# Six denominator products a quad for eight, with two pair sums merged by an accumulating DMA

## The chip, the cores and the metric

One core of a Trainium2 chip runs the kernel. The metric is the device time of one execution in microseconds; the profile comes from one profiled execution of the same program.

## The reference

For each of 8 batches, `x` and `ctx` are 512 rows by 1024 columns. The kernel computes a gated cross attention over the 1024 columns with 16 heads of 32 rows each, and then a gated product whose operands are rounded to an 8-bit float:

```
x = x + tanh(g_xattn) * attention(layernorm(x), ctx, mask)       # 16 heads, softmax over the 1024 source columns
x = x + tanh(g_ffn) * (fp8(layernorm(x) * scale) / scale) @ (fp8(W2 * scale1) / scale1)
```

Inside the attention, `q`, `k` and `v` are projections with bias, the scores are divided by the root of 32, masked, and put through a softmax. Its denominator is the sum of the exponentials over all 1024 source columns.

## The kernel before, in words

A first stage (to about 570 us) projects every batch's `q`, `k` and `v` and stores them in DRAM. The second stage walks through 32 quads, `n`: four heads (128 rows) of one batch. A quad is a period of 64 slots, `k`. All five engines have the same list of slots written out by hand, and each does in a slot what the program lists for it.

- In slot `k` TensorE (PE) multiplies one 128 x 512 tile of scores (`scores`, L863) and one tile of unshifted scores for the maxima of the quad after it (`scores_for_max`, L878). ScalarE (ACT) takes the exponential of the first (`exp`, L715), VectorE (DVE) the maximum of the second (`maximum`, L1143). A slot's head is `k % 4`, and four slots make one chunk of 128 source columns. Slots 0 to 31 serve the first half of the target columns (`th` = 0), 32 to 63 the second.
- After every fourth slot (`k % 4 == 3`) PE multiplies a chunk of exponentials with `v` (`times_v`, L893).
- GpSimd (POOL) adds the chunks pairwise: pair `r` is made of the exponentials of slots 8r to 8r+7, one 128 x 512 addition for each head (`add_pair`, L398). Its four additions need the exponentials of slots 8r+4 to 8r+7. They go to one of two buffers of `pair_sum`.
- PE sums a pair's rows into the denominator's bank with a product by ones (`denominators`, L904): 4 instructions in the code, 8 records in the trace, one after every eighth slot: pair `r` at slot 19 + 8r, so pair 0 at slot 19, pair 1 at slot 27, pair 7 at slot 75, which is slot 11 of the period after.
- At slots 23 and 55 PE turns the maxima's negated high and low parts (`turn_max`, L933), ACT copies them and SyncE's queue (SP) sends them into the score operand (`set_max`), which the scores of slots 32 and 64 need. At slots 31 and 47 PE does the fp8 product of two quads before (`ffn`, L940).
- The inverse denominators go through SP's queue: `move_den`, the reciprocal on DVE (L1168, L1171), `move_inv`, `spread_inv`. POOL multiplies with them (`weigh`, L407) and adds the residual (`add_residual`, L413) behind pair 3. POOL also has one power of a single column (L427) behind pair 4.

## Time and profile before

| | |
|---|---|
| Median of 3 runs | 2501.88 us (2497.44 to 2505.27) |
| The profiled execution's own time | 2498.55 us |
| Its span | 2496.9 us |
| PE busy | 2441.7 us, 98% of the span |
| DVE busy | 1960.7 us, 79% |
| POOL busy | 1643.2 us, 66% |
| ACT busy | 1387.1 us, 56% |
| Mean granted TensorE clock | 0.996 |

Busy time is the union of an engine's instructions; matmuls overlap in the records, so a single record (0.40 us) is longer than the distance between two (0.23 us). The distances between starts are what a reader should take as PE's pace. POOL's issue of a DMA would not be counted as busy.

### The profile page before, as it was taken

To read this page: it belongs to the slowest core of one execution; us is meant where nothing else is said; L and a number is where in the kernel's file an instruction comes from. 1 tells how busy PE (TensorE), PEld (TensorE's weight loads), DVE (VectorE), ACT (ScalarE), POOL (GpSimd) and SP (SyncE) were. 2 spreads that over 40 slices of the span, in tenths; PEclk is the share of its full clock that TensorE was granted. 3 is DMA by queue.
4 is the path that set the end of the run, shared out by engine and by line. 5 is a ranking of instruction groups with operands and counts; after the bars stand their busy time and mean duration, and the time that the engine had idled before them with its cause. 6 is when DMAs were issued, how large, how long until landed. Compare 5 with 4: busy or idle time off the path is not lost.

```text
span 2496.9 us, 40504 instructions
## 1 busy us (share of the span) xinstructions
PE 2441.7 (98%) x13116; PEld 1382.0 (55%) x13177; DVE 1960.7 (79%) x3259; ACT 1387.1 (56%) x2606; POOL 1643.2 (66%) x1259
## 2 busy tenths in 40 slices
PE   7999999999999999999999999999999999999997
PEld 5888888875444444444444444444444444444442
DVE  6677776687788888888888888888888888888885
ACT  3333333315666666666666666666666666666664
POOL 2443333426777777777777777777777777777775
PEclk9999999999999999999999999999999999999999
DMA  6766666664444444444444444444444444444411
GB/s 245 262 243 237 234 235 235 227 188 100 94 102 98 102 101 102 97 94 95 94 93 100 92 92 92 92 92 101 92 93 95 99 101 102 98 101 97 104 45 56
DMA packets 241807, 313.48 MB, mean 126 GB/s; under 512 B 75000, under 2 KB 142648, under 8 KB 241624
## 3 DMA queue, kind: packets, MB, share of 16 engines
q1 hardware_dynamic: 230776, 275.56, 44.0%
q10 hardware_dynamic: 10848, 35.66, 4.0%
q8 instruction: 93, 1.52, 0.3%
q14 instruction: 90, 0.74, 0.1%
HBM read 199.83 MB, written 101.38 MB: 121 GB/s over the span
## 4 chain that ended last, share of the span: by engine, by line
PE 94%; DVE 1%; DMA 1%; issue 1%; POOL 1%; ACT 1%; SPq 0%; POOLq 0%; ACTq 0%; DVEq 0%
PE bank L863 22%; PE bank L893 20%; PE bank L848 20%; PE bank L878 19%; PE bank L904 9%; PE bank L940 4%; PE bank L933 1%; POOL pair_sum L398 1%; DMA q_st<-qx_scr 0%; DMA w_nat<-in_L_xattn_Wk_dram 0%; DMA v_scr<-stage 0%; ACT probs L715 0%; DVE x_raw L1043 0%; PE bank L802 0%; PE bank L924 0%
## 5 line engine op out<-in xcount | busy, mean ns | idle before, releaser
L398 POOL TENSOR_TENSOR pair_sum<-probs 128x512 f32<-128x512 f32 x1020 | 1279.2, 1286 | 399.0 <-ACT probs L715 399.0
L1143 DVE TENSOR_REDUCE part_max<-bank 128x1 f32<-128x512 f32 x2048 | 1276.6, 682 | 242.7 <-PE bank L878 229.2
L715 ACT ACTIVATE probs<-bank 128x512 f32<-128x512 f32 x2048 | 1067.4, 604 | 601.7 <-PE bank L863 578.7
L863 PE MATMUL bank<-q_st,k_st 100*128 100x512 f32 x2048 | 866.3, 425 | 6.0 <-ACT probs L715 6.0
L878 PE MATMUL bank<-k_st,q_st 98*128 98x512 f32 x2048 | 817.4, 399 | 8.3 <-DVE part_max L1143 6.5
L863 PEld LDWEIGHTS bank<-q_st,k_st 100*128 100x128 f32 x2048 | 387.4, 190 | 410.3 <-issue 211.2
L893 PE MATMUL bank<-probs,v_t 128*32 128x512 f32 x4096 | 545.6, 605 | 0.0
L878 PEld LDWEIGHTS bank<-k_st,q_st 98*128 98x128 f32 x2048 | 388.7, 190 | 129.2 <-DVE part_max L1143 15.8
L389 POOL TENSOR_TENSOR stage_lo<-stage,stage_hi 128x512 fp32r<-128x512 f32 x128 | 186.6, 1483 | 137.7 <-ACT stage_hi L661 136.2
L904 PE MATMUL bank<-pair_sum,ones 128*32 128x512 f32 x2040 | 265.5, 592 | 0.0
L661 ACT ACTIVATE stage_hi<-stage 128x512 fp32r<-128x512 f32 x128 | 80.2, 633 | 205.1 <-DVE stage L1007 142.9
L377 POOL TENSOR_TENSOR rstd<-ve,neg_half 128x4 f32<-128x4 f32 x8 | 14.6, 1830 | 230.7 <-DVE ve L1038 230.7
L893 PEld LDWEIGHTS bank<-probs,v_t 128*32 128x32 f32 x4096 | 80.8, 108 | 146.6 <-issue 92.8
L904 PEld LDWEIGHTS bank<-pair_sum,ones 128*32 128x32 f32 x2040 | 66.4, 110 | 152.5 <-issue 151.0
L1195 DVE SCALAR_TENSOR_TENSOR res<-bank,g,res 128x512 f32<-128x512 f32 x64 | 47.9, 750 | 112.3 <-PE bank L940 108.6
L940 PE MATMUL bank<-w2q,y_t 128*128 128x512 bf16 x435 | 103.9, 379 | 10.1 <-issue 9.6
L696 ACT ACTIVATE stage<-stage,sm_now 128x512 f32<-128x512 f32 x64 | 44.6, 720 | 119.3 <-DVE stage L1003 119.2
L848 PE MATMUL bank<-w_hi_v,c_hi 128*128 128x512 f32 x256 | 101.3, 396 | 4.2 <-DVE w_lo_q L1056 4.2
L848 PE MATMUL bank<-c_hi,w_hi_k 128*128 128x512 f32 x256 | 100.0, 390 | 1.4 <-DVE w_lo_k L1056 1.4
L848 PE MATMUL bank<-w_hi_v,c_lo 128*128 128x512 f32 x256 | 101.2, 395 | 0.0
L848 PE MATMUL bank<-w_lo_v,c_hi 128*128 128x512 f32 x256 | 100.8, 394 | 0.0
L848 PE MATMUL bank<-x_hi,w_hi_q 128*128 128x512 f32 x256 | 99.9, 390 | 0.0
(112 smaller groups left out, 2007.3 us busy)
## 6 DMA issues: line engine op xcount, KB each, us to landing
k_st<-k_scr SPq DMA_DIRECT2D x96, 512.0 KB
q_st<-q_scr SPq DMA_DIRECT2D x192, 256.0 KB
c_raw<-in_ctx_dram ACTq DMA_DIRECT2D x32, 512.0 KB, 7.0
k_scr<-stage_hi SPq DMA_DIRECT2D x64, 256.0 KB, 2.5
k_scr<-stage_lo SPq DMA_DIRECT2D x64, 256.0 KB, 2.7
v_scr<-stage SPq DMA_DIRECT2D x64, 256.0 KB, 2.9
q_scr<-stage_hi SPq DMA_DIRECT2D x64, 256.0 KB, 2.4
q_scr<-stage_lo SPq DMA_DIRECT2D x64, 256.0 KB, 2.7
```

What stands on the lines that cost most here:

```text
L389: nc.gpsimd.tensor_tensor(stage_lo[:, e % STG], stage[:, g % STG], stage_hi[:, e % STG].bitcast(F32), ALU.subtract).then_inc(qk_lo, 1)
L398: nc.gpsimd.tensor_tensor(pair_sum[:, r % 2, h], probs[:, a, h], probs[:, a + 1, h], ALU.add).then_inc(pair_done, 1)
L661: nc.scalar.activation(stage_hi[:, e % STG], stage[:, g % STG], ACT.Copy).then_inc(qk_hi, 1)
L715: nc.scalar.activation(probs[:, c % PR, h, :], s_bank_of(n, k)[:, :], ACT.Exp).then_inc(exp_done, 1)
L848: last = nc.tensor.matmul(acc, a, m, start=(cb == 0 and n == 0), stop=(cb == CB - 1 and n == 2))
L863: nc.tensor.matmul(s_bank_of(n, k)[:, :], k_st[p][0:KS, h, j * P:(j + 1) * P], q_st[p][0:KS, th, h, :], start=True, stop=True).then_inc(sc ...
L878: nc.tensor.matmul(x_bank_of(n, "tile", k)[:, :], q_st[p][0:KX, th, h, tc * P:(tc + 1) * P], k_st[p][0:KX, h, sh * HALF:(sh + 1) * HALF], ...
L893: last = nc.tensor.matmul(o_bank[D * h:D * (h + 1), :], v_t[p][:, j, D * h:D * (h + 1)], probs[:, c % PR, h, :], start=(j == 0), stop=(j = ...
L904: last = nc.tensor.matmul(d_bank[D * h:D * (h + 1), :], ones[:, :], pair_sum[:, r % 2, h, :], start=(i == 0), stop=(i == 3))
L940: last = nc.tensor.matmul(x_bank_of(n, f"ffn{half}", k)[:, :], y8_t[:, kc, :], w2q[:, kc, half * HALF:(half + 1) * HALF], start=(kc == 0), ...
L1143: nc.vector.tensor_reduce(part_max[:, th, sh, at:at + 1], x_bank_of(n, "tile", k)[:, :], AX, ALU.max).then_inc(max_done, 2)
L1195: nc.vector.scalar_tensor_tensor(res[p][:, s], x_bank_of(n, f"ffn{half}", k)[:, :], g2[:, 0:1], res[p][:, s], ALU.mult, ALU.add).then_inc( ...
```

## The change

- Denominators: six products for each quad and not eight. POOL issues a DMA that adds the sum of pair 0 onto that of pair 1 (and pair 4 onto pair 5), 128 rows of 2048 floats, in SBUF (`merge`). There are four buffers of sums now; the two new ones are the first stage's `stage` and `stage_hi`. The order is pair 2 at slot 27, the merged pair 0+1 at slot 35, pair 3 at slot 43, pair 6 at slot 59, the merged pair 4+5 at slot 67 (3 of the next period), pair 7 at slot 75 (11).
- The maxima's split: DVE's three small operations become reductions, with a copy on ACT (`minus_high`) between them, spread over slots 19 to 22 (51 to 54); the sign moves to the identity.
- The inverse's mask goes to POOL (`mask_inverse`), its gate factor to ACT (`mask_gates`); the reciprocal moves from slots 23 and 55 to 19 and 51. In SP's queue `set_max` stands ahead of `move_inv`, and the loads of `q` are split by half.
- On POOL the weighing is done in halves, behind pair 2 and behind pair 3; the power stands inside pair 5. The fp8 products stand at slots 39 and 51, and DVE's last two rounding steps at 27.

The core of the diff:

```diff
+            sums = [pair_sum[:, 0], pair_sum[:, 1], stage[:, :, :], stage_hi[:, :, :].bitcast(F32)]
...
-            F_JOBS = {23: "max1", 31: "ffn0", 47: "ffn1", 55: "max0"}
+            F_JOBS = {23: "max1", 39: "ffn0", 51: "ffn1", 55: "max0"}
+            DEN_AT = {27: 0, 35: 1, 43: 2, 59: 3}
+            DEN_AFTER = {3: 4, 11: 5}
+            NG = 6
+            SUM_OF_GROUP = (2, 1, 3, 6, 5, 7)
+            GROUP_OF_SUM = {1: 1, 2: 0, 3: 2, 5: 4, 6: 3, 7: 5}
+            MERGED = (0, 4)
...
-            FFN_AT = (31, 47)
+            FFN_AT = (39, 51)
...
+                    def wait_sum_free(n, r):
+
+                        m, was = (n, r - 4) if r >= 4 else (n - 1, r + 4)
+                        if m < 0:
+                            return
+                        if was in MERGED:
+                            pool.wait_ge(merged[was // 4], 16 * (m + 1))
+                        else:
+                            pool.wait_ge(den_done, NG * m + GROUP_OF_SUM[was] + 1)
...
                     def add_pair(n, r):
                         a = 2 * r % PR
-                        if counted(SJ * n + r - 1):
-                            pool.wait_ge(den_done, SJ * n + r - 1)
+                        wait_sum_free(n, r)
                         for h in range(QH):
+                            if (r, h) == (5, 1) and n > 0:
+                                invert_std_2(n - 1)
                             pool.wait_ge(exp_done, NSLOT * n + 2 * QH * r + QH + h + 1)
-                            nc.gpsimd.tensor_tensor(pair_sum[:, r % 2, h], probs[:, a, h], probs[:, a + 1, h],
+                            nc.gpsimd.tensor_tensor(sums[r % 4][:, h], probs[:, a, h], probs[:, a + 1, h],
                                                     ALU.add).then_inc(pair_done, 1)
...
+                    def merge(n, th):
+
+                        pool.wait_ge(pair_done, QH * (SJ * n + 4 * th + 2))
+                        pool.dma_start(sums[1], sums[0], accum_op=ALU.add).then_inc(merged[th], 16)
...
                     def period(n, p):
                         for r in range(SJ):
+                            if n == 0 and r == 0:
+                                wait_stage_free()
                             if real(n) and (n, r) != (LAST, SJ - 1):
                                 add_pair(n, r)
+                            if real(n) and r % 4 == 1:
+                                merge(n, r // 4)
+                            if r == 2 and ordinary(n - 1):
+                                mask_inverse(n - 1, 1)
+                                weigh(n - 1, 0)
+                            if r == 6 and real(n):
+                                mask_inverse(n, 0)
                             if r == 3 and ordinary(n - 1):
-                                weigh(n - 1)
+                                weigh(n - 1, 1)
                                 add_residual(n - 1, 1 - p)
...
-                    def denominators(m, r):
-                        th, i = r // 4, r % 4
+                    def denominators(m, g):
+                        th, i = g // 3, g % 3
+                        r = SUM_OF_GROUP[g]
                         if i == 0:
                             if counted(2 * m + th):
                                 pe.wait_ge(den_copied, 2 * m + th)
-                        pe.wait_ge(pair_done, QH * SJ * m + QH * (r + 1))
+                        if i == 1:
+                            pe.wait_ge(merged[th], 16 * (m + 1))
+                        else:
+                            pe.wait_ge(pair_done, QH * SJ * m + QH * (r + 1))
```

PE's program around slots 19 to 27, of before: the products with `v` after slot 23, the turn of the maxima, then the products with `v` after slot 27 and the denominator's. The slots' own tiles (L863, L878) are left out.

```order
L893 MATMUL bank3<-probs,v_t1 32x512 [waits exp_done]
L893 MATMUL bank3<-probs,v_t1 32x512 x3
L933 MATMUL bank6<-ident_r,neg_max 128x128 [waits max_done,negmax_done]
...
L893 MATMUL bank3<-probs,v_t1 32x512 [waits exp_done]
L893 MATMUL bank3<-probs,v_t1 32x512 x3
L904 MATMUL bank4<-pair_sum,ones 32x512 [waits pair_done]
L904 MATMUL bank4<-pair_sum,ones 32x512 x3
```

The same place of the change, from the products after slot 23 to the denominator's product at slot 27 and the one at slot 35.

```order
L989 MATMUL bank3<-probs,v_t0 32x512 [waits exp_done]
L989 MATMUL bank3<-probs,v_t0 32x512 x3
L1033 MATMUL bank6<-neg_ident,max_hl 128x128 [waits max_done,max_split]
...
L989 MATMUL bank3<-probs,v_t0 32x512 [waits exp_done]
L989 MATMUL bank3<-probs,v_t0 32x512 x3
L1004 MATMUL bank4<-stage,ones 32x512 [waits pair_done,den_copied]
L1004 MATMUL bank4<-stage,ones 32x512 x3
...
L1004 MATMUL bank4<-pair_sum,ones 32x512 [waits merged0]
L1004 MATMUL bank4<-pair_sum,ones 32x512 x3
```

At slot 27 stood the product of pair 1; now pair 2 (in `stage`) stands there, the first of its half. No product stands at slot 19 any more, and the one at slot 35 waits for the merging DMA.

POOL's program of before, from pair 2 of a period to pair 4:

```order
L398 TENSOR_TENSOR pair_sum<-probs 128x512 [waits exp_done,den_done]
L398 TENSOR_TENSOR pair_sum<-probs 128x512 [waits exp_done] x3
L398 TENSOR_TENSOR pair_sum<-probs 128x512 [waits exp_done,den_done]
L398 TENSOR_TENSOR pair_sum<-probs 128x512 [waits exp_done] x3
L407 TENSOR_TENSOR y<-o_raw,inv_b 128x1024 [waits inv_spread,o_copied]
L413 TENSOR_TENSOR res<-res,y 128x1024 [waits res_loaded0,norm_done]
L398 TENSOR_TENSOR pair_sum<-probs 128x512 [waits exp_done,den_done]
L398 TENSOR_TENSOR pair_sum<-probs 128x512 [waits exp_done] x3
L427 TENSOR_TENSOR rs<-ve,neg_half 128x1 [waits norm_done]
```

POOL's program of the change, from the end of pair 1 to the residual behind pair 3:

```order
L441 TENSOR_TENSOR pair_sum<-probs 128x512 [waits exp_done] x3
L447 DMA pair_sum<-pair_sum 128x2048 [waits pair_done]
L441 TENSOR_TENSOR stage<-probs 128x512 [waits exp_done,den_done]
L441 TENSOR_TENSOR stage<-probs 128x512 [waits exp_done] x3
L425 TENSOR_TENSOR inv_c<-inv_c,gtm_c 128x16 [waits gates_masked,inv_done]
L462 TENSOR_TENSOR y<-o_raw,inv_b 128x512 [waits inv_spread0,o_copied]
L441 TENSOR_TENSOR stage_hi<-probs 128x512 [waits exp_done,den_done]
L441 TENSOR_TENSOR stage_hi<-probs 128x512 [waits exp_done] x3
L462 TENSOR_TENSOR y<-o_raw,inv_b 128x512 [waits inv_spread1,o_copied]
L469 TENSOR_TENSOR res<-res,y 128x1024 [waits res_loaded0,norm_done,half_weighed]
```

The merging DMA is issued between pair 1 and pair 2, and the mask and the first half of the weighing come between pair 2 and pair 3.

## Rows read from the trace of the kernel before

**Rows 1.** Windows, steady stage: busy us by engine, clock, DMA share, GB/s

```profile
1000.00:1500.00 500.00, 496.56 (x2813) 245.38 (x2829) 408.84 (x717) 310.85 (x609) 381.62 (x294) 1.00 0.43 94
```

**Rows 2.** Waits of PE, whole span: total us, times, longest

```profile
PE bank L878 <- DVE part_max L1143: 6.5, 3, 5.0
```

**Rows 3.** The page's groups: busy, mean ns, idle before and its releaser

```profile
L398 POOL TENSOR_TENSOR pair_sum<-probs 128x512 f32<-128x512 f32 x1020 | 1279.2, 1286 | 399.0 <-ACT probs L715 399.0
L1143 DVE TENSOR_REDUCE part_max<-bank 128x1 f32<-128x512 f32 x2048 | 1276.6, 682 | 242.7 <-PE bank L878 229.2
L904 PE MATMUL bank<-pair_sum,ones 128*32 128x512 f32 x2040 | 265.5, 592 | 0.0
```

**Rows 4.** Timeline from slot 20 of one period: start, us, engine, line

```profile
1536.62 0.50 PE L863 MATMUL bank<-q_st,k_st 100*128 100x512 f32 x1
1537.24 2.06 ACT L715 ACTIVATE probs<-bank 128x512 f32<-128x512 f32 x4 [1.87 <-PE bank L863]
...
1537.98 5.02 POOL L398 TENSOR_TENSOR pair_sum<-probs 128x512 f32<-128x512 f32 x4 [1.98 <-ACT probs L715]
...
1539.68 0.33 PE L933 MATMUL bank<-ident_r,neg_max 128*128 128x128 f32 x1
...
1541.86 1.06 PE L893 MATMUL bank<-probs,v_t 128*32 128x512 f32 x8
...
1542.74 1.04 PE L904 MATMUL bank<-pair_sum,ones 128*32 128x512 f32 x8
1543.71 0.51 PE L863 MATMUL bank<-q_st,k_st 100*128 100x512 f32 x1
...
1547.01 1.67 PE L940 MATMUL bank<-w2q,y_t 128*128 128x512 bf16 x7 [0.16 <-issue]
```

**Rows 5.** Timeline, slots 60 to 64 (no denominator between) and slot 12

```profile
1515.66 0.50 PE L863 MATMUL bank<-q_st,k_st 100*128 100x512 f32 x1
...
1517.73 1.07 PE L893 MATMUL bank<-probs,v_t 128*32 128x512 f32 x8
1518.72 0.50 PE L863 MATMUL bank<-q_st,k_st 100*128 100x512 f32 x1
...
1529.63 0.50 PE L863 MATMUL bank<-q_st,k_st 100*128 100x512 f32 x1
...
1530.99 5.01 POOL L398 TENSOR_TENSOR pair_sum<-probs 128x512 f32<-128x512 f32 x4 [1.96 <-ACT probs L715]
```

**Rows 6.** Timeline, last period: POOL's additions, a waiting weight load, DVE

```profile
2440.36 4.97 POOL L398 TENSOR_TENSOR pair_sum<-probs 128x512 f32<-128x512 f32 x4 [1.38 <-ACT probs L715]
...
2445.49 0.13 PEld L904 LDWEIGHTS bank<-pair_sum,ones 128*32 128x32 f32 x4 [0.30 <-POOL pair_sum L398]
...
2463.16 7.41 POOL L398 TENSOR_TENSOR pair_sum<-probs 128x512 f32<-128x512 f32 x4 [2.64 <-ACT probs L715]
```

**Rows 7.** DMA issues: count, KB each, median us from issue to landing

```profile
v_t<-v_scr SPq DMA_DIRECT2D x32, 512.0 KB, 4.1
...
w_nat<-in_L_xattn_Wk_dram SPq DMA_DIRECT2D x1, 1024.0 KB, 10.3
```

**Rows 8.** Windows of 2 us inside the burst of loads

```profile
1524.00:1526.00 2.00, 2.00 (x13) 0.75 (x12) 1.97 (x4) 1.33 (x3) 1.99 (x2) 1.00 1.05 222
1526.00:1528.00 2.00, 2.00 (x12) 1.30 (x15) 1.45 (x3) 1.67 (x4) 2.00 (x3) 1.00 1.03 141
```

**Rows 9.** SP's own rows in that period: issue time of each DMA

```profile
1517.60 1.30 SPq L498 DMA_DIRECT2D k_st<-k_scr  x3
...
1531.36 0.56 SPq L518 DMA_DIRECT2D den_c<-den  x1
```

**Rows 10.** POOL's power of four columns, and DVE's small operation late once

```profile
L377 POOL TENSOR_TENSOR rstd<-ve,neg_half 128x4 f32<-128x4 f32 x8 | 14.6, 1830 | 230.7 <-DVE ve L1038 230.7
...
2431.71 0.57 DVE L1152 TENSOR_TENSOR row_max<-part_max 128x16 f32<-128x16 f32 x1
...
2432.32 0.17 DVE L1157 TENSOR_SCALAR neg_max<-row_max 128x16 fp32r<-128x16 f32 x1
```

More of the change, by code:

```diff
@@ L176, in flamingo_gated_layer @@
         init_done = sem("init_done")
-        stacked = [sem(f"stacked{i}") for i in range(TH)]
+        k_stacked = sem("k_stacked")
+        q_stacked = [sem(f"q_stacked{i}") for i in range(TH)]
         v_loaded = [sem(f"v_loaded{i}") for i in range(2)]
@@ L187, in flamingo_gated_layer @@
         pair_done = sem("pair_done")
+        merged = [sem(f"merged{i}") for i in range(TH)]
         pv_done = sem("pv_done")
@@ L193, in flamingo_gated_layer @@
         inv_done = sem("inv_done")
+        gates_masked = sem("gates_masked")
         inv_moved = sem("inv_moved")
-        inv_spread = sem("inv_spread")
+        inv_spread = [sem(f"inv_spread{i}") for i in range(TH)]
         tm_loaded = sem("tm_loaded")
         res_loaded = [sem(f"res_loaded{i}") for i in range(2)]
+        half_weighed = sem("half_weighed")
         norm_done = sem("norm_done")
@@ L588, in period @@
                             load_v(n + 1, 1 - p)
+                        if real(n) and real(n + 2):
+                            stack_q(n + 2, 0, p)
                         if real(n):
@@ L727, in copy_den, with minus_high @@
                         nc.scalar.activation(den[:, :], d_bank[:, :], ACT.Copy).then_inc(den_copied, 1)
+                    def minus_high(m, th):
+                        act.wait_ge(max_split, 4 * (2 * m + th) + 2)
+                        nc.scalar.activation(row_max[:, :, 1], max_hl[:, 0:QH * TC].bitcast(F32), ACT.Copy,
+                                             scale=-1.0).then_inc(max_split, 1)
                     def copy_max(n, m, th, k):
@@ L756, in normalize, with mask_gates @@
                                              scale=rss[:, 0:1]).then_inc(norm_done, 1)
+                    def mask_gates(m):
+                        act.wait_ge(tm_loaded, 16 * TH * (m + 1))
+                        if m == 0:
+                            act.wait_ge(chain_done, 1)
+                        if counted(4 * m):
+                            act.wait_ge(inv_done, 4 * m)
+                        nc.scalar.activation(gtm_c[:, :, :], tm_c[:, :, :], ACT.Copy, scale=g1[:, 0:1]).then_inc(gates_masked, 1)
                     def period(n, p):
@@ L761, in period @@
                                 exp(n, k)
+                            if k == 46 and real(n):
+                                mask_gates(n)
                             if k == 3 and ordinary(n - 1):
@@ L765, in period @@
                                 copy_den(n - 1, 1)
+                            if k == 20 and real(n):
+                                minus_high(n, 1)
+                            if k == 52 and real(n + 1):
+                                minus_high(n + 1, 0)
                             if k == 23 and real(n):
@@ L785, in _ @@
                     act.wait_ge(ident_done, 2)
-                    nc.scalar.activation(ident_r[:, :], ident_f[:, :], ACT.Copy).then_inc(ident_copied, 1)
+                    nc.scalar.activation(neg_ident[:, :], ident_f[:, :], ACT.Copy, scale=-1.0).then_inc(ident_copied, 1)
                     split_ctx(0)
```

196 lines of the change are left out of this document (112 added, 84 removed).

## The prediction

> **What bounds the kernel now.** I read the windows of the steady stage first: of 500 us PE is busy in 496.6, at a granted clock of 1.00 (its upper level, 2.4 GHz), DVE in 409, POOL in 382, ACT in 311 [rows 1]. The waits say the same from the other side: in the whole span PE waited 6.5 us for DVE's maxima, its longest wait for another engine's tiles [rows 2]. So in 32 periods PE sets the time: what leaves PE's list leaves the time, and what makes PE wait is added. POOL and DVE have room on average, but both run close to PE: POOL's groups wait 399 us in all for exponentials [rows 3], about 12 us a period, so a wait of PE for POOL would be decided by single slots.
>
> **What is removed.** One denominator product. From the products with `v` at slot 27 to the next slot's tile it is 1541.86 to 1543.71, 1.85 us, with a denominator between [rows 4], and 1517.73 to 1518.72, 0.99 us, without [rows 5]. So one costs PE 0.86 us. The page counts 2040 records, 255 products of 8 [rows 3]; two leave each of 32 quads, 64 in all: 64 x 0.86 = **-55.0 us**. The other products, the tiles and the fp8 products only change places.
>
> **The wait at slots 27 and 59.** The first product of each half is now that of pair 2 (pair 6). Its four additions follow the exponentials of slots 20 to 23, and it stands at slot 27. Before, pair 1 stood there, finished at 1530.99 + 5.01 = 1536.00 [rows 5], 6.7 us before PE came. In the row POOL starts pair 2 at 1537.98, 1.36 us behind slot 20's tile at 1536.62, and needs 5.02: it ends at 1543.00. PE came to the product at 1542.74 [rows 4]. Between slot 20 and slot 27 the change leaves PE's list as it was (4 + 4 slots, one turn), so PE comes as early as before, and must wait. From POOL's end to the weight load that waits there is the row of the last period: 2440.36 + 4.97 = 2445.33, load at 2445.49, 0.16 us [rows 6]; a load takes about 0.1. So the product starts at 1543.00 + 0.16 + 0.1 = 1543.26 for 1542.74, 0.5 us late. Slots 52 to 59 are the same list, so the same wait. It comes about 62 times (the last quad has no tiles beside it): 62 x 0.5 = **+31 us**. The bounds of this wait: 0.26 (POOL's end alone) gives +16, and 0.8, if the new reductions of the maxima or ACT's new copy hold the chain up a little, gives +50. DVE's last reduction of the split comes behind slot 22 for the turn after slot 23; if that is late by 0.1 or 0.2 us it is inside this wait, not beside it.
>
> **The issue of the merging DMA on POOL.** No DMA is issued from POOL before, so its price D is unknown. Behind pair 1 it delays pair 2. From slot 12 to slot 20 PE takes 1536.62 - 1529.63 = 6.99 us [rows 4, 5], less the 0.86 of slot 19's product: 6.13. POOL's four additions take 5.01 [rows 5], so 1.1 us are free and only D - 1.1 is added at slot 27. Below stands SP's issue, 1.30 us for three, 0.43 each [rows 9]; above, POOL's own slowest small operation, 1.83 us [rows 10]. I take 1.3, since software on POOL is nearer to the second, which adds 0.2 us in 31 periods: **+6 us**; the ends are 0 and 31 x 0.7 = +22. Behind pair 5 the fp8 product at slot 51 (at least 1.6 us [rows 4]) makes room for D and for the power, so nothing is added there. The Trainium skill (DMA: Bandwidth & Descriptors, Specifications) gives about 1 us to the first byte of a DMA issued from GpSimd; D by that would be under 1.1 and this term zero.
>
> **The merging DMA itself.** It starts when pair 1 is done, 1.36 + 5.01 = 6.4 us behind slot 12's tile. Slot 35's product comes at 6.13 + 6.12 + 0.5 + 0.98 + 6.0 = 19.7, so it may take 13.3 us with its issue. For pair 4+5: the additions and the power end 7.0 us behind slot 44, slot 67's product comes at 6.12 + 1.6 + 6.12 + 0.5 + 0.98 + 6.0 = 21.3: 14.3 us. It moves 1.05 MB and reads two such tiles. Rows for its price: 512 KB in 4.1 us, so 1 MB in 8; 1 MB among other loads in 10.3 [rows 7]; 2.1 MB read at the burst's 222 GB/s, 9.4 [rows 8]. The burst of the next quad's loads (issued from 1517.60 on, behind slot 63 [rows 9]) is 3.2 MB, 15 us at 222 GB/s and 23 at 141 [rows 8]; half of `q` is loaded later now, which leaves 2.4 MB, 11 to 17 us, over when pair 1 is done at slot 20, 18 us on. I take 10 to 11 us and **0 us**. The bounds: 8, and 3.15 MB (two reads, one write) at the burst's slow 141 GB/s, 22 us, which would cost (8.7 + 7.7) x 31 = +508. If cover is gone, each microsecond over both limits costs 62 us.
>
> **The rest, all at nothing.** DVE has 0.58 us free in four slots without a denominator (3.06 us from 1515.66 to 1518.72 [rows 5], less four maxima of 0.62 each), and its larger steps now stand at slots that keep a product (3, 11, 27, 43, 59) or an fp8 product. The reciprocal at slot 19 waits for `den_c`, issued at 1531.36, slot 13 to 14 [rows 9]; the loads ahead of it in the queue are now a quarter less, so it lands before slot 19. If not, DVE's maxima stop, and PE three tiles later. ACT has 1.0 us free in such a group (four exponentials in 2.06 [rows 4]) and gets one small copy at slots 20, 46 and 52. `set_max` now leaves earlier in SP's queue. POOL gets two masks and two halves for one weighing; after pair 2 they end before slot 28's exponential by my count, after pair 3 the residual makes pair 4 about 2 us late, and pair 5 catches up. The last period has no maxima, so PE is not full there and POOL's line decides: two issues, and the merged pair 4+5 which PE wants some 6 us after its issue and gets after 10. Part of that is covered by DVE's own backlog; I take **+4 us**, bounds 0 and 10.
>
> **Sum** against the profiled execution's own 2498.55 us: -55 + 31 + 6 + 0 + 4 = -14, so 2484.5. The median of the runs lies 3.3 us above that execution, so on its scale **2488 us**, a ratio of 0.994. What a measurement of this kernel can tell from no change is about 0.3%, 7.5 us.
>
> **The rivals.** *The merging DMA is too slow* (the other side). Place: slots 35 and 67. It decides from the point where both latenesses together eat 14/31 = 0.45 us a period, a duration of about 13.7 to 14 us; at 15 it is (1.7 + 0.7) x 31 = +74, 2562 us. For it: two reads, an arithmetic step nowhere seen in this trace. Against it: 1 MB in 8 to 10.3 [rows 7], and DMA engines busy 0.43 of the time on average [rows 1].
>
> *The issue is long*, D of 2.2 us or more, by its own work or by a lock. POOL's additions show that it can be held up: four took 7.41 us in the last period for 5 elsewhere [rows 6], while DVE worked on pairs of SBUF inputs, and DVE's 16-column operation took 0.57 us once, its neighbour 0.17 [rows 10]. At D = 2.2 the term is 31 x 1.1 = +34 for +6: 2516 us, slower. Against it: at slots 20 and 52 DVE has only maxima from PSUM and small reductions in its list. The Trainium skill (SBUF — State Buffer, Who interferes with whom) says that descriptors of a DMA issued from GpSimd starve while DVE runs in a two-port mode, and that reductions never contend on trn2; by that rule this case does not come up at these two slots.
>
> *No wait at slots 27 and 59*, because POOL's recorded ends, which the page calls rough, are late and its signal comes earlier, or a short D and the last period cost nothing: -55 + 0 to 15, 2450 to 2462 us. For it: that note. Against it: a waiting load of the last period came 0.16 us behind POOL's recorded end, not before it [rows 6].
>
> *It does nothing*: DVE or POOL takes over as the bound and fills the 1.7 us a period. For it: DVE 82% and POOL 76% busy [rows 1], of a shorter period 84% and 80% with the issues. Against it: both still wait. Time 2495 to 2505.
>
> **How the numbers follow.** My forecast, waits of half a microsecond twice a period and a hidden transfer: 0.52, its own range 2468 to 2508 (0.42 of it faster by over 0.3%, 0.08 within, 0.02 slower). No wait: 0.16, faster. Slow transfer: 0.13, slower. Long issue: 0.11, of which 0.02 within and 0.09 slower. Nothing: 0.08, of which 0.04 within, 0.02 either side. Faster 0.60, same 0.14, slower 0.26. The low end takes in most of the case without a wait, 2454; the high end the long issue and the mild part of a slow transfer, 2525.
>
> **What would show it.** Denominator records 1528 for 2040; PE's distance from `v`'s products to the next tile 0.99 us at slots 19 and 51. A wait of PE's weight load for POOL's additions of about 0.4 to 0.5 us, 62 times, and none for the merging DMA outside the last period. POOL's idle time ahead of pair 2 near zero. A period of about 58.9 us for 59.4 (16 x 3.06 + 8 x 0.86 + 2 x 1.6, and two turns of some 0.2). I am wrong if PE's waits name the DMA, if POOL starts pair 2 more than 0.3 us behind slot 20's exponential, or if PE waits for DVE at slots 20 to 24.

## The result and the profile after

The change makes the kernel slower: 2543.81 us median (2535.99 to 2553.53, 4 runs) for 2500.11 us (2497.44 to 2505.27, 4 runs) on the same chip, a ratio of 1.0174 with an interval of [1.0129, 1.0219]. The profiled execution took 2553.53 us, the longest of its four, with a span of 2551.7 us and a mean granted clock of 0.980. It lies 10 us above the median, so sums below are made against its own span.

First the windows of the steady stage, in the columns of [rows 1]: the first line answers to its line there, the others are three stretches of 3 us.

```profile
1000.00:1500.00 500.00, 485.08 (x2635) 238.92 (x2651) 396.86 (x690) 310.46 (x622) 389.32 (x328) 0.98 0.64 130
1326.00:1329.00 3.00, 3.00 (x8) 1.93 (x6) 1.39 (x4) 2.09 (x5) 1.92 (x2) 0.50 1.08 233
1329.00:1332.00 3.00, 3.00 (x12) 1.05 (x12) 1.28 (x3) 0.67 (x2) 3.00 (x3) 0.50 0.56 115
1332.00:1335.00 3.00, 3.00 (x20) 1.70 (x22) 2.40 (x5) 2.17 (x4) 0.23 (x2) 0.89 0.07 11
```

PE is no longer full: 485 us busy of 500, and even DVE has less to do in 500 us than before, so the whole line moves more slowly. The clock column reads 0.98. In the second and third line it is 0.50, the lower of its two levels (1.2 GHz for 2.4), although PE is busy in all 3 us. DMA went from 94 to 130 GB/s.

Lines picked from the waits over the whole span (us in total, times, longest) say for what PE, DVE, POOL and SyncE's queue wait:

```profile
DVE inv_c L1270 <- DMA den_c<-den: 41.2, 22, 4.3
PE bank L974 <- DMA k_st<-kx_scr: 21.0, 15, 1.9
PE bank L974 <- DVE part_max L1242: 20.0, 16, 4.8
POOL pair_sum L441 <- DMA q_scr<-stage_lo: 19.0, 1, 19.0
POOL pair_sum L447 <- POOL pair_sum L441: 18.8, 63, 0.3
PE bank L957 <- ACT probs L786: 17.4, 11, 14.1
PE bank L1004 <- POOL stage L441: 10.2, 19, 3.6
SPq L597 <- DMA inv_scr<-inv_c: 115.4, 63, 3.2
```

No wait of PE for the merging DMA is in the list. What PE waits for is the loads of `k` for the maxima's scores (L974), 15 times, and DVE's maxima, 16 times; DVE in turn waits 22 times at its reciprocal (L1270) for `den_c`. Before, PE waited for the maxima 3 times and 6.5 us [rows 2], and its list had no wait for `k_st`. The last line is of SyncE's queue, where the same wait of the inverse's spread was much shorter before:

```profile
SPq L528 <- DMA inv_scr<-inv_c: 22.5, 62, 1.7
```

The merging DMA, from the page (its issues, KB each, median us from issue to landing) and from its own line's view:

```profile
pair_sum<-pair_sum POOLq DMA_DIRECT2D x64, 1024.0 KB, 7.4
L447 POOL DMA_DIRECT2D pair_sum<-pair_sum x64: 867/884/1057, 603.1 to 2506.6; - x64
DMA to landing us min/median/max: 6.9/7.4/10.2
```

It holds POOL for 0.88 us, after a wait of 0.30 us for the pair before it, and lands after 7.4 us.

**Where the time went.** The turn of the maxima (L1033, L933 before) stands twice a period, behind slots 23 and 55, so the distances between its 64 starts are a ruler for the second stage. Read from those starts, with the stage cut at the third turn and at the last but one (60 halves between them), in us:

| kernel | start to third turn | 60 halves | rest | span |
|---|---|---|---|---|
| before | 617.4 | 1790.5 | 89.1 | 2496.9 |
| after | 633.5 | 1819.7 | 98.5 | 2551.7 |

So 16 us are lost ahead of the third turn, 29 in the steady stage and 9 at the end. Within the steady stage halves are of two kinds. Where nothing is late they take 27.58 us (slot 55 to 23) and 31.1 us (23 to 55), a period of 58.7 us for 59.7 by the same ruler: shorter, as forecast. The others are longer by up to 5 us. One of these is the half from the turn at 1298.88; the view of windows for it and for the half after it:

```profile
1298.88:1331.05 32.17, 30.10 (x157) 14.42 (x153) 24.40 (x41) 18.33 (x36) 23.32 (x21) 0.92 0.81 166
1331.05:1362.46 31.41, 31.09 (x172) 15.75 (x170) 23.75 (x44) 19.90 (x40) 24.23 (x21) 0.97 0.38 80
```

It takes 32.17 us where an undisturbed one takes 27.58, 4.6 us more, with 2.1 us of idle PE; the next one still has a clock of 0.97. Its chain of waits, in order of time (start, us, what):

```profile
1302.13 0.19 POOL inv_c L425
...
1302.34 3.25 DMA inv_scr<-inv_c
...
1305.61 0.56 SPq L597
...
1306.27 0.42 SPq L560
...
1307.68 16.45 DMA k_st<-kx_scr
...
1324.17 0.49 PE bank L974
```

and what POOL, PE and DVE show there on the timeline:

```profile
1323.92 0.88 POOL L447 DMA_DIRECT2D pair_sum<-pair_sum  x1 [0.30 <-POOL pair_sum L441]
1324.17 0.49 PE L974 MATMUL bank<-k_st,q_st 98*128 98x512 f32 x1 [1.93 <-DMA k_st<-kx_scr]
...
1326.01 0.63 PE L974 MATMUL bank<-k_st,q_st 98*128 98x512 f32 x1
...
1327.61 0.25 DVE L1270 RECIPROCAL inv_c<-den_c 128x16 f32<-128x16 f32 x1 [1.81 <-DMA den_c<-den]
```

POOL's mask of the inverse (L425) stands behind pair 6. SyncE's queue waits for it, sends the inverse to DRAM (3.25 us for 8 KB, where the same transfer took 1.4 us in the median before), then issues the spread (L597), and only behind that the loads of the next quad's `k` and `q` (L560): 7.4 us behind the turn. In the halves without loss it is 6.3 us, before it was 6.0. These loads land 1.9 us after PE wants them. Then PE runs at half clock, its matmul records 0.63 us for 0.40, to 1332: six microseconds at 0.50 are 3 us lost, more than the wait that went before. In 11 of the 30 periods the distance to the turn is 7.2 us or more (up to 7.7), and PE waits for `k_st` in each of them; in four others, issued at 6.3 to 6.9 us, it waits 0.6 to 1.2 us.

What made the chain late can be read from SyncE's rows. The kernel before, behind its turn at 1271.89:

```profile
1272.77 0.33 SPq L522 DMA_DIRECT2D inv_scr<-inv_c  x1
...
1274.19 0.54 SPq L528 DMA_DIRECT2D inv_b<-inv_scr  x1
1277.87 1.30 SPq L498 DMA_DIRECT2D k_st<-k_scr  x3
```

The change, behind its turn at 1298.88, has the maxima's transfer first:

```profile
1299.54 0.69 SPq L616 DMA_DIRECT2D q_st<-max_rows  x1
```

The inverse left 0.9 us behind the turn before and leaves 3.5 us behind it now (1302.34). The spread stood ahead of the loads in the kernel before too, with 3 us to spare. SyncE's queue waits for POOL's mask 56 times (115.7 us), so it is the mask's place behind pair 6, much more than the place of `set_max`, that made the inverse late; the second kernel below tells the two apart.

The clock did not fall behind every such wait. In after and in the second, fourth and ninth kernels below, all eight single waits of PE of 1.9 us or more in the 60 halves were followed by 3 to 10 us at 0.50; of those from 1.4 to 1.9 us some were and some were not (1.64 us at 1866.88 was, 1.76 us at 1746.60 was not).

### The profile page after: what moved, and what is told of

The parts are those of the page before. It is cut to its first block, busy times and chain, and to the rows that moved or that the text cites. A ratio compares the mean times of both kernels' runs of the same rounds, so it can differ in the third digit from the quotient of the medians.

```text
span 2551.7 us, 39827 instructions
## 1 busy us (share of the span) xinstructions
PE 2436.1 (95%) x12604; PEld 1374.4 (54%) x12665; DVE 1937.0 (76%) x3196; ACT 1406.7 (55%) x2702; POOL 1718.8 (67%) x1417
## 4 chain that ended last, share of the span: by engine, by line
PE 74%; DMA 9%; POOL 9%; issue 4%; DVE 2%; ACT 2%; SPq 1%; ACTq 0%; POOLq 0%; DVEq 0%
PE bank L942 20%; PE bank L957 16%; PE bank L989 14%; PE bank L974 13%; PE bank L1004 6%; POOL stage L441 6%; DMA den_c<-den 5%; PE bank L1040 4%; POOL pair_sum L441 3%; DMA k_st<-kx_scr 3%; ACT probs L786 1%; DMA q_scr<-stage_lo 1%; DMA inv_scr<-inv_c 0%; DVE part_max L1242 0%; DMA w_nat<-in_L_xattn_Wk_dram 0%
## 5 line engine op out<-in xcount | busy, mean ns | idle before, releaser
L786 ACT ACTIVATE probs<-bank 128x512 f32<-128x512 f32 x2048 | 1081.2, 603 | 634.7 <-PE bank L957 605.9
L957 PE MATMUL bank<-q_st,k_st 100*128 100x512 f32 x2048 | 876.9, 430 | 17.6 <-ACT probs L786 17.4
L974 PE MATMUL bank<-k_st,q_st 98*128 98x512 f32 x2048 | 829.0, 405 | 41.4 <-DMA k_st<-kx_scr 21.0
L441 POOL TENSOR_TENSOR pair_sum<-probs 128x512 f32<-128x512 f32 x512 | 642.2, 1283 | 184.9 <-ACT probs L786 165.8
L957 PEld LDWEIGHTS bank<-q_st,k_st 100*128 100x128 f32 x2048 | 392.9, 192 | 428.7 <-issue 226.8
L989 PE MATMUL bank<-probs,v_t 128*32 128x512 f32 x4096 | 554.9, 614 | 0.0
L974 PEld LDWEIGHTS bank<-k_st,q_st 98*128 98x128 f32 x2048 | 393.4, 192 | 172.6 <-DVE part_max L1242 44.0
L441 POOL TENSOR_TENSOR stage_hi<-probs 128x512 f32<-128x512 f32 x252 | 316.3, 1288 | 78.6 <-ACT probs L786 78.6
L441 POOL TENSOR_TENSOR stage<-probs 128x512 f32<-128x512 f32 x256 | 324.2, 1313 | 57.1 <-ACT probs L786 57.0
L390 POOL TENSOR_TENSOR rstd<-ve,neg_half 128x4 f32<-128x4 f32 x8 | 14.7, 1831 | 233.1 <-DVE ve L1137 233.1
L462 POOL TENSOR_TENSOR y<-o_raw,inv_b 128x512 f32<-128x512 f32 x62 | 80.0, 1291 | 79.7 <-DVE y L101 71.0
L1293 DVE SCALAR_TENSOR_TENSOR res<-bank,g,res 128x512 f32<-128x512 f32 x64 | 47.9, 750 | 103.4 <-PE bank L1040 98.2
```

The source lines that it names most:

```text
L441: nc.gpsimd.tensor_tensor(sums[r % 4][:, h], probs[:, a, h], probs[:, a + 1, h], ALU.add).then_inc(pair_done, 1)
L462: nc.gpsimd.tensor_tensor(y[:, th * HALF:(th + 1) * HALF], o_raw[:, th], inv_b[:, th], ALU.mult).then_inc(done, 1)
L786: nc.scalar.activation(probs[:, c % PR, h, :], s_bank_of(n, k)[:, :], ACT.Exp).then_inc(exp_done, 1)
L957: nc.tensor.matmul(s_bank_of(n, k)[:, :], k_st[p][0:KS, h, j * P:(j + 1) * P], q_st[p][0:KS, th, h, :], start=True, stop=True).then_inc(sc ...
L974: nc.tensor.matmul(x_bank_of(n, "tile", k)[:, :], q_st[p][0:KX, th, h, tc * P:(tc + 1) * P], k_st[p][0:KX, h, sh * HALF:(sh + 1) * HALF], ...
L989: last = nc.tensor.matmul(o_bank[D * h:D * (h + 1), :], v_t[p][:, j, D * h:D * (h + 1)], probs[:, c % PR, h, :], start=(j == 0), stop=(j = ...
```

## The experiments

Every kernel is compared with before on its own chip. The table holds all of them, each profiled execution cut as above; the rows are explained below.

| kernel | median us | ratio to before | to third turn | 60 halves | rest |
|---|---|---|---|---|---|
| after | 2543.8 | 1.0174 [1.0129, 1.0219] | 633.5 | 1819.7 | 98.5 |
| buffer wait later (e1) | 2539.0 | 1.0158 [1.0141, 1.0175] | 630.6 | 1802.4 | 98.1 |
| mask earlier (e2) | 2516.1 | 1.0060 [1.0043, 1.0077] | 637.9 | 1784.2 | 94.5 |
| reciprocals later (e3) | 2525.1 | 1.0104 [1.0081, 1.0128] | 634.6 | 1791.5 | 97.9 |
| no merges (e4) | 2505.0 | 1.0024 [1.0011, 1.0036] | 637.7 | 1773.9 | 98.2 |
| e1 + e2 + e3 (e5) | 2636.2 | 1.0535 [1.0517, 1.0552] | 630.5 | 1903.9 | 100.3 |
| e5 + spread behind loads (e6) | 2636.3 | 1.0543 [1.0526, 1.0561] | 629.2 | 1900.4 | 100.4 |
| e6 + stores first (e7) | 2633.9 | 1.0532 [1.0514, 1.0550] | 625.0 | 1902.4 | 100.5 |
| small merges (e8) | 2521.7 | 1.0089 [1.0071, 1.0107] | 633.3 | 1788.5 | 96.3 |
| e5, first reciprocal back (e9) | 2505.8 | 1.0014 [1.0003, 1.0025] | 631.3 | 1783.7 | 93.3 |
| e9 + spread behind loads (e10) | 2486.9 | 0.9940 [0.9923, 0.9956] | 631.7 | 1760.3 | 94.1 |
| e10 + stores first (e11) | 2481.2 | 0.9918 [0.9902, 0.9935] | 626.6 | 1759.8 | 94.0 |
| spread behind loads alone (e12) | 2504.9 | 1.0018 [1.0008, 1.0028] | 633.4 | 1771.8 | 97.1 |
| e11 without merges (e13) | 2480.3 | 0.9911 [0.9893, 0.9929] | 626.9 | 1757.4 | 95.4 |

The fourth, eighth and thirteenth kernels leave sums, or most of their columns, out of the denominators: they are for timing only.

**One edit at a time.** The first moves POOL's wait for the first stage's buffers from pair 0 to pair 2 of the first quad, where `stage` is first written:

```diff
-                            if n == 0 and r == 0:
+                            if n == 0 and r == 2:
                                 wait_stage_free()
```

> One edit to the changed kernel: the first quad's wait for the stage buffers stands ahead of pair 2, which is the first to write one, and not ahead of pair 0. Theory A (the changed kernel lost 14.1 us of PE time once, in the first quad, because GpSimd's pair 0 waited 19.0 us for the last stores of q, which stand in SP's queue behind 3.2 MB of loads): the first step from turn to turn falls from 43.7 us to about 29 to 30, the run to about 2529 us for 2543.8. Rival (the first quad is late for another reason, the loads themselves): the wait moves to pair 2, slot 27, and less than 4 us are won.

2539.0 us, 5 us less, not 15, and the two intervals overlap: nearer to the rival. The first half of the stage fell from 43.7 to 32.6 us, the second rose from 28.5 to 37.5. POOL's pair 2 now waited 10.7 us for the same transfer, `q_scr<-stage_lo`. The stores of the first stage are what is late, and they stand in SyncE's queue behind the second quad's loads. (Its 60 halves are 17 us shorter than after's; nothing in the edit explains that. I take it for the spread between executions, which is 17.5 us from the fastest to the slowest of after; it is not shown.)

The second puts the mask of the first half's inverse behind pair 5:

```diff
-                            if r == 6 and real(n):
+                            if r == 5 and real(n):
                                 mask_inverse(n, 0)
```

> One edit to the changed kernel: GpSimd's mask of the first half's inverse stands behind pair 5 and not behind pair 6, about seven slots earlier. Theory B (SP's queue, which stands at the inverse's transfers until about a microsecond after slot 63, issues the next quad's loads of k too late, so that PE waits for them at slot 19; 21 us in 15 waits): the loads go out right behind slot 63 in every period, PE's waits for k go from 21 us to under 5, and DVE's waits for the denominators' copy at slot 19 (41 us in 22) shrink too, since it stands behind the same loads; 2505 to 2520 us. Rival C (the merging DMA's traffic slows the loads): the waits for k stay above 15 us and the time within 8 us of 2543.8.

2516.1 us, 28 less. PE's waits for `k_st` fell from 21.0 us in 15 to 11.8 in 9, those of DVE for `den_c` from 41.2 to 22.1: the loads go out 7.2 us or more behind the turn in 6 of 30 periods, for 11 in after, and what comes behind them in the queue with them. Theory B has the time, but not the waits under 5 us. SyncE's rows behind the turn at 1285.29 show why:

```profile
1286.69 1.19 SPq L589 DMA_DIRECT2D inv_scr<-inv_c  x1
1292.06 0.56 SPq L597 DMA_DIRECT2D inv_b<-inv_scr  x1
1292.71 1.55 SPq L560 DMA_DIRECT2D k_st<-k_scr  x3
```

The inverse now leaves 1.4 us behind the turn, 2.1 us earlier, though `set_max` still stands ahead of it. But its small transfer takes a median of 3.6 us, for 2.0 in after, and eats most of what was won.

The third puts both reciprocals back to slots 23 and 55, behind the fp8 step's addition:

```diff
-                        if k == 19 and ordinary(n - 1):
+                        if k == 23 and ordinary(n - 1):
                             invert(n - 1, 1)
-                        if k == 51 and real(n):
+                        if k == 55 and real(n):
                             invert(n, 0)
```

> One edit to the changed kernel: DVE's reciprocal stands at slots 23 and 55 again and not at 19 and 51. Theory D (DVE's wait for the denominators' copy at slot 19, 41 us in 22 waits, holds back the maxima and by them PE: PE's 20.0 us in 16 waits for DVE): these waits go to zero, PE's waits for k stay at about 21 us; 2520 to 2530 us. Rival B (both waits have the late loads as their one cause, and PE, when it is held at slot 19 by k, loses nothing more by DVE): under 8 us are won.

2525.1 us, 19 less. DVE's wait for `den_c` is gone and with it PE's for the maxima but one; PE's wait for `k_st` stays at 19.9 us in 13. So the reciprocal is a cause of its own, theory D.

The fourth takes the merging DMA away, its issue, traffic and both waits for it:

```diff
-                            if real(n) and r % 4 == 1:
-                                merge(n, r // 4)
...
-                        if i == 1:
-                            pe.wait_ge(merged[th], 16 * (m + 1))
-                        else:
-                            pe.wait_ge(pair_done, QH * SJ * m + QH * (r + 1))
+                        pe.wait_ge(pair_done, QH * SJ * m + QH * (r + 1))
```

> The changed kernel without its two merging DMAs a quad; the sums of pairs 0 and 4 are left out of the denominators, the rest is as it was. Theory C (the 67 MB that the merges move, and their issue of 0.9 us on GpSimd, slow SP's small transfers and the loads of k): the inverse's small transfer takes 1.4 us again for up to 3.3, PE's waits for k fall below 5 us and the run to about 2505 to 2515. Rival B (the order in SP's queue and on GpSimd alone is at fault): the waits for k stay, and the time within 8 us of 2543.8.

2505.0 us, 39 less, though PE never waits for the merge: waits for `k_st` 8.8 us in 5 (theory C had them under 5 us), for the maxima 9.2 in 7, `den_c` 15.1 in 11. The small transfer of the inverse is back at a median of 1.4 us (2.0 in after). So the merge does most of its harm through others' transfers. It is not alone in that: in five periods the small transfer took 2.9 to 3.5 us without any merge, and these are the five in which PE waited for `k_st`. What slows it there was not tested. The eighth kernel cuts the merges to 32 of 512 columns, a sixteenth of the traffic with the same issues on POOL:

```diff
-                        pool.dma_start(sums[1], sums[0], accum_op=ALU.add).then_inc(merged[th], 16)
+                        pool.dma_start(sums[1][:, :, 0:32], sums[0][:, :, 0:32], accum_op=ALU.add).then_inc(merged[th], 16)
```

> The changed kernel with the two merging DMAs a quad reduced to a sixteenth of their columns (32 of 512 for each head; the rest of the sums of pairs 0 and 4 is left out of the denominators). GpSimd still issues 64 of them. Traffic theory (what the merges cost is their 67 MB beside the loads): the time is that without the merges, about 2505 us. Issue theory (what they cost is the 0.9 us on GpSimd and the wait for the pair before it): the time stays within 10 us of 2540.

2521.7 us, between the two theories: 22 us of the 39 go with the traffic and 17 remain with the issues. The waits say where: for `k_st` they are those of the fourth kernel (9.4 us in 5), but DVE waits for `den_c` 28.8 us in 24, for 15.1 in 11, and PE for the maxima 14.7 in 19, for 9.2 in 7. Why the issue alone does that stays open.

**Three edits together, and a stall of their own.** The fifth kernel has the first three edits at once. The sixth adds an edit to SyncE's queue (below), the seventh one more.

> The three edits of the runs before together: the stage wait ahead of pair 2, the mask of the first half's inverse behind pair 5, the reciprocal at slots 23 and 55. If the late loads of k and the wait for the denominators' copy are two causes (won alone: 28 us and 19 us), both are gone and what is left is PE's wait for k where the loads were out in time but slow: 2500 to 2508 us, the changed kernel's waits for k about 12 us as with the mask alone. If they are one cause, it does no better than the mask alone, 2512 to 2518 us.

> As the run of three edits, and SP's queue issues the spreading of the first half's inverse (256 KB) behind the loads of k and q of the next period and not ahead of them. Theory B (SP's place in its queue decides when k is issued): every issue of k comes 6.3 us behind the turn at slot 55, none at 7 or more, PE's waits for k fall from about 12 us to under 5, and the time lies 5 to 12 us under the run of three edits. Theory C (the merge of pairs 4 and 5 and the other traffic slow the loads even when issued in time): the issue is in time, but waits of 5 us or more stay.

> As the run before it, and the loads for quad 1 stand in SP's queue behind the first stage's last two pairs of stores and not ahead of them. With the wait only moved to pair 2, the first two half periods still took 70.1 us for about 59 in the kernel before; if the stores behind 3.2 MB of loads are the cause, they land about 15 us earlier and the two half periods take 59 to 62 us, 8 to 11 us less in the run; the price, loads 3 to 5 us later, costs at most 4 us at slot 19. Rival: the loads for quad 1 are what the first period waits for, and nothing is won.

All three missed by far: 2636.2, 2636.3 and 2633.9 us (ratios in the table). The waits of the fifth show why, and it is not the kernel's fault but the combination's:

```profile
PE bank L1004 <- POOL stage L441: 117.0, 63, 7.1
POOL inv_c L425 <- DVE inv_c L1270: 105.2, 32, 3.9
```

The mask stands behind pair 5, some slot 52, and now waits on POOL for a reciprocal at slot 55; pair 6 stands behind it, and PE waits for pair 6 at slot 59. The waits for `k_st` and `den_c` are gone, but under this stall neither the sixth nor the seventh could show what its own edit is worth. Only one thing could be read: with the stores ahead, the first two halves took 64.2 us for 68.6 in the sixth.

So the ninth to eleventh repeat the ladder with the first half's reciprocal left at slot 51, where the mask finds it done:

```diff
                         if k == 51 and real(n):
                             invert(n, 0)
...
                         if k == 23 and ordinary(n - 1):
                             invert(n - 1, 1)
```

> The first stage's buffer wait ahead of pair 2, the inverse's mask behind pair 5, the reciprocal of the second half at slot 23 and that of the first half left at slot 51, so that the mask finds it done. The stall of 117 us of PE for POOL's tiles in 63 products, which the three edits together had made, should be gone. Theory A (causes of their own that add up: mask 28 us, reciprocal 19, buffer wait 5): 2543.8 - 52 = 2492 us, ratio to before 0.997, no wait of DVE for den_c at the second half, PE's waits for k_st under 12 us. Theory B (mask and reciprocal are two ends of the same lateness, and the merging DMAs' own traffic and issue keep a part): 2504 to 2512 us, ratio 1.002 to 1.005.

2505.8 us, 38 less than after, in theory B's range. Seven waits for `k_st` stay:

```profile
PE bank L974 <- DMA k_st<-kx_scr: 12.4, 7, 2.3
```

The tenth moves the spread of the first half's inverse behind the next period's loads, in SyncE's queue:

```diff
                         if n > 0 and real(n + 1):
                             stack_k(n + 1, 1 - p)
                             stack_q(n + 1, 1, 1 - p)
                         if ordinary(n - 1):
+                            spread_inv(n - 1, 0)
                             move_den(n - 1, 1)
...
                         if real(n):
                             move_inv(n, 0)
+                        if n == LAST:
                             spread_inv(n, 0)
```

> As the kernel before it in this list, and in the queue of SyncE the spread of the first half's inverse stands behind the next period's loads of k and q. Theory A (the loads of k still stand behind the inverse's chain for a part of the periods): PE's waits for k_st fall to 0 to 3 us, and the time by 5 to 10 us against the kernel before it. Theory B (once the mask is early the loads are on time, and what is left comes from the merges' traffic): the same time within 4 us.

2486.9 us, 19 less than the ninth and faster than before. The direction is theory A's, its size twice to four times what I gave: seven waits of 12.4 us in all were worth 23 us in the 60 halves, 3.3 us each, since I had again left out the clock: PE is idle 10 us less there, and its busy time is 13 us shorter, with no half below a clock of 1.00 where the ninth has five. Its windows in the steady stage, in the columns of [rows 1]:

```profile
1000.00:1500.00 500.00, 496.57 (x2745) 244.34 (x2742) 409.36 (x715) 320.08 (x645) 408.64 (x341) 1.00 0.66 134
```

PE is as full as before the change and at full clock, with DMA at 134 GB/s.

The eleventh moves the second quad's loads behind the first stage's last stores:

```diff
-                            if not more and g == G - 2:
-                                sp.wait_ge(group_done, B * G)
-                                stack_k(1, 1)
-                                stack_q(1, 0, 1)
-                                stack_q(1, 1, 1)
...
+                        if not more:
+                            sp.wait_ge(group_done, B * G)
+                            stack_k(1, 1)
+                            stack_q(1, 0, 1)
+                            stack_q(1, 1, 1)
```

> As the second of this list, and the loads of the second quad stand behind the first stage's last stores in the queue of SyncE. Theory A (in the first period only the queue's order holds POOL's pair 2 back): the first two halves of the second stage take 60 to 64 us for about 70, and the whole time is 5 to 9 us below the second of this list, so 2480 to 2500 us. Theory B (the first period is held by ScalarE's exponentials and the stores' traffic as well): 0 to 3 us less.

2481.2 us, 5.7 less, as theory A had it, though the first two halves still take 65.3 us: POOL no longer waits for the stores, but the loads come later in turn:

```profile
PE bank L976 <- DMA q_st<-qx_scr: 7.2, 1, 7.2
PE bank L1006 <- POOL stage L441: 13.5, 42, 1.3
```

**The queue's order alone, and the merges alone.** The twelfth is the changed kernel with the tenth's edit to the queue and nothing else:

> The changed kernel with one edit: in the queue of SyncE the spread of the first half's inverse stands behind the next period's loads of k and q, not ahead of them. Mask, reciprocals and buffer wait stay where the change put them. Theory A (the lateness does harm only because the loads stand behind the inverse's chain): the waits of PE for k_st and for part_max and of DVE for den_c, 21 and 20 and 41 us, all but disappear, and the time is 2543.8 less 40 to 50, so 2494 to 2504 us. Theory B (the early mask is needed by itself, and so is the late reciprocal): 2515 to 2530 us, with den_c still waited for 20 us or more.

2504.9 us, 39 less, the time at the edge of theory A; but of its three waits only one goes:

```profile
PE bank L976 <- DVE part_max L1244: 21.6, 26, 5.0
DVE inv_c L1272 <- DMA den_c<-den: 35.3, 31, 4.3
```

Every wait for `k_st` is gone, and the loads are issued 6.3 to 6.6 us behind the turn in all periods, since the spread (L597) is now issued behind them. SyncE's rows behind the turn at 1279.59:

```profile
1283.06 0.34 SPq L589 DMA_DIRECT2D inv_scr<-inv_c  x1
1285.93 1.28 SPq L560 DMA_DIRECT2D k_st<-k_scr  x3
...
1289.68 0.56 SPq L597 DMA_DIRECT2D inv_b<-inv_scr  x1
```
The waits for `den_c` stay, in nearly every period, as theory B had it; but they hold PE for 1.3 us at most each in the 60 halves, and the clock stays at 1.00: a half with 0.9 us of such a wait takes 28.76 us, 1.2 more than an undisturbed one, where in after one with 1.9 us took 4.6 more. So the loads standing behind the inverse's chain are what cost 39 us, and the early reciprocal is a second cause. The mask's place loses its weight once no load is behind it, since the twelfth without that edit has no late load either. The order in which the spread precedes the loads is as in the kernel before; the change made it harmful by letting the chain end later. What the 18 us between the twelfth and the tenth kernel owe to the reciprocal, the mask and the buffer wait, each alone, was not measured in this order of the queue.

The thirteenth is the eleventh without merges (the edit of the fourth):

> The best version so far (early mask, the second half's reciprocal at slot 23, spread behind the loads, loads of the second quad behind the first stage's stores, buffer wait ahead of pair 2) with the merging DMAs left out, so the sums of pairs 0 and 4 are missing from the denominators. Theory A (the merges' traffic did harm only through the small transfers that the loads waited for): 2478 to 2481 us, within 4 us of the same kernel with merges, PE's waits for POOL at slots 27 and 59 shorter by what the issue of 0.9 us took. Theory B (the merges still hold up loads, stores or POOL): 2465 to 2475 us.

2480.3 us, within 1 us of the same kernel with merges, as theory A had it. The halves from slot 23 to 55 take 31.03 us for 31.09, so the issues cost POOL and PE at most 0.06 us each; PE's waits for POOL did not shorten (14.3 us in 49, for 13.5 in 42), against that part of the theory. With no load behind the small transfer, 1 MB of merging each half period costs 2.4 us in the 60 halves and nothing that the medians show. So the 39 us of the fourth kernel and the 39 us of the twelfth are the same microseconds, won back at two ends.

## Why the prediction was wrong

The time came out 56 us above the 2488 that were forecast, and on the other side of the kernel before.

*What held.* The removed products: a half without any wait at slot 27 takes 30.65 us in the twelfth for 31.55 before, 0.9 us less (0.86 forecast). The merging DMA lands in 7.4 us (10 to 11 assumed, 8 the lower bound), well inside its 13 us, and no wait of PE names it. The period of undisturbed halves is 58.7 us for a forecast of 58.9; but by the same ruler the kernel before takes 59.7 and not 59.4, so a period without lateness gains 1.0 us and not 0.5. The issue takes 0.88 us on POOL for the 1.3 assumed, so the term of +6 is near zero. The Trainium skill's figure that was weighed there (about 1 us to the first byte of a DMA issued from GpSimd, DMA: Bandwidth & Descriptors, Specifications) pointed that way, though it is the time to a first byte and not the hold on POOL. The rival of a long issue did not come up: the 64 issues lie between 0.867 and 1.057 us, so none was held up by DVE. The Trainium skill's rule against contention (SBUF — State Buffer, Who interferes with whom) agrees with that.

*What was a little too large.* The wait at slots 27 and 59: +31 was forecast, 0.5 us twice a period. PE's rows in the eleventh, from the products with `v` to the next slot's tile, at slot 59 and at slot 27:

```profile
1330.80 1.06 PE L991 MATMUL bank<-probs,v_t 128*32 128x512 f32 x8
...
1332.99 0.50 PE L959 MATMUL bank<-q_st,k_st 100*128 100x512 f32 x1
...
1358.39 1.07 PE L991 MATMUL bank<-probs,v_t 128*32 128x512 f32 x8
...
1360.70 0.50 PE L959 MATMUL bank<-q_st,k_st 100*128 100x512 f32 x1
```

These are 2.19 and 2.31 us, for 1.85 before [rows 4]: 0.34 and 0.46 us late, although the records call only 0.26 us of it a wait for POOL. For 31 periods that is +25. With two products gone and 0.8 us of this wait, the 30 periods of the 60 halves should be 27 us shorter than before; in the eleventh they are 30.7 shorter, for 17 by the forecast's -55, +31 and +6.

*What failed.* The step "The rest, all at nothing", in two places. One said that the reciprocal's `den_c` "lands before slot 19": DVE waited for it 22 times in after and 31 times in the twelfth. I had argued from the bytes ahead of it in the queue, which became fewer, and gave the four slots by which the reciprocal came nearer no number: they are 3.3 us (28.3 us behind the turn at slot 55 before, 25.0 now), and in the twelfth the 8 KB issued 20.1 us behind the turn at 1279.59 let DVE start only at 26.5. The other counted POOL's masks and `set_max` as work and as a place in a queue, and asked nothing about what then leaves later: the inverse's move and spread, and behind them the next quad's loads. The move left 2.6 us later; the mask's place behind pair 6 made 2.1 of it and `set_max` ahead of it at most 0.5, as the second kernel shows. I had taken the loads of `k` as "over when pair 1 is done" for the merge's sake, without asking how much margin PE has for them. It was next to nothing: issued 6.3 us behind the turn they are mostly in time, at 6.9 PE waits 0.6 us, at 7.2 to 7.7 it waits 1.1 to 1.9. My own list of what would show it wrong had "if PE waits for DVE at slots 20 to 24"; the waits came there and at slot 19, for `k_st` as much as for DVE.

Two costs stood nowhere in the sum. The clock: a wait of 1.9 us brought it to 0.50 for some 6 us, which more than doubles what it cost. The 60 halves of after took 60 us more than the eleventh's: PE was idle 40 us more (53.2 for 13.6), and its busy time was 20 us longer (1766.6 for 1746.1) at the lower clock. And the first quad: POOL waits 19 us for the buffers that the first stage still stores from, +16 us ahead of the third turn, of which the eleventh's order gives back 7; I had read `stage` and `stage_hi` as free without looking at when their last stores land. At the end +4 was forecast and +9 came: DVE's reciprocal waits 4.3 us for `den_c`, and PE 3.6 us for pair 6 (before [rows 6] four additions took as long).

```profile
2507.80 7.52 POOL L441 TENSOR_TENSOR stage<-probs 128x512 f32<-128x512 f32 x4 [0.32 <-ACT probs L786]
...
2515.47 1.94 PE L1004 MATMUL bank<-stage,ones 128*32 128x512 f32 x8 [3.58 <-POOL stage L441]
```

With the lateness repaired the gain from the removed products shows: 2481 us for the 2488 predicted, a version 0.8% faster than before and 2.5% faster than the change. That the two numbers lie so close is partly luck: the steady stage gained 31 us where 17 were forecast, and the first quad, for which nothing was forecast, took 9 us of that back.

## What to carry to other kernels

When an item in a queue is moved ahead, list everything behind it up to the next load that the bottleneck engine wants, and read from the trace how many tenths of a microsecond that load has to spare; here a load with less than 1 us to spare stood behind a chain of POOL, a small transfer and a wait, and 39 us hung on the order of two lines. Ask it of every producer in that chain: here the mask moved to another engine's list, and no line of the queue shows that. A DMA that no engine waits for can still cost, by making small transfers in front of something else slower; here the remedy was the order, not the DMA. An edit that pulls a consumer earlier must be checked against where its producer stands now, or it makes a stall of its own, as the fifth kernel did.

## What the runs showed of the hardware

A wait of PE of 1.93 us was followed by 6 us at a granted clock of 0.50 though PE was busy throughout; so were the seven others of 1.9 us or more in after and the second, fourth and ninth kernels, for 3 to 10 us. Of those between 1.4 and 1.9 us some were and some were not. The waits of the twelfth's 60 halves, 1.33 us at the longest, left it at 1.00. An accumulating DMA from SBUF to SBUF of 1 MB, issued by POOL, held it for 0.88 us and landed in 7.4 us (6.9 to 10.2). The 8 KB transfer of the inverse took 1.4 us in the median before (up to 2.9), 2.0 in after (up to 3.6), 3.6 in the second kernel, where it left 2 us earlier (up to 6.9), and 1.4 in the fourth without merges (up to 3.5). Another 8 KB, `den_c`, took 6.3 us from its issue to DVE's reciprocal in one period of the twelfth (1299.72 to 1306.07), behind the next quad's loads.
